# Norms with tokens on partitions, and another opening and ending of the last attention, in a fused four-block transformer kernel

## The reference, cut to what matters

```python
def _layernorm(x, axis=-1, eps=1e-05):
    m = jnp.mean(x, axis=axis, keepdims=True)
    v = jnp.var(x, axis=axis, keepdims=True)
    return (x - m) / jnp.sqrt(v + eps)
...
        Q = _l2norm(Qp)          # first attention: x / max(sqrt(sum x^2), 1e-12)
...
        # last attention, 16 heads of 8
        q = (query @ Wq + bq).reshape(B, Nq, H, D).transpose(0, 2, 1, 3)
        k = (key_value @ Wk + bk).reshape(B, Nkv, H, D).transpose(0, 2, 1, 3)
        v = (key_value @ Wv + bv).reshape(B, Nkv, H, D).transpose(0, 2, 1, 3)
        attn = jnp.einsum('bhqd,bhkd->bhqk', q, k) * scale
        attn = jnp.clip(attn, -CLAMP, CLAMP)
        attn = jax.nn.softmax(attn, axis=-1)
        attn = jnp.where(jnp.any(jnp.isnan(attn)), jnp.asarray(1.0 / Nkv, attn.dtype), attn)
        x = jnp.einsum('bhqk,bhkd->bqhd', attn, v).reshape(B, Nq, Cq)
        return x @ Wo + bo
```

## Time and profile before

| | us |
|---|---|
| median of the timed runs (three, 4366.15 to 4369.79) | 4366.79 |
| the profiled execution, its own time | 4373.3 |
| its span in the profile | 4371.7 |
| busy PE, DVE, ACT, POOL | 3678.5, 2638.5, 2052.6, 1419.1 |
| last attention, first clip to last copy | 3436.9 to 4284.0 |

### The profile page before, as it was taken

The page is one execution under the profiler, slowest core; times in us unless marked ns, Lnnn a source line. Parts: engine busy times, 40 slices in busy tenths (PEclk is TensorE's granted clock), DMA queues, the critical chain, the costliest instruction groups (busy, mean ns, idle before and its releaser), DMA issues. The chain is left out here.

```text
span 4371.7 us, 85152 instructions
## 1 busy us (share of the span) xinstructions
PE 3678.5 (84%) x32894; PEld 2444.3 (56%) x32894; DVE 2638.5 (60%) x3505; ACT 2052.6 (47%) x2955; POOL 1419.1 (32%) x1888
## 2 busy tenths in 40 slices
PE   7389999936279999988999997589777799989986
PEld 7267777613246666654666664267533366656663
DVE  8656666553244555425555543467545899989993
ACT  7267777701014344432443442266422477767763
POOL 0164555122422322212233220022102556656630
PEclk9689999968669999998999997799888799999997
DMA  6167777445132333312333320011001666666640
GB/s 168 49 154 171 179 170 174 116 162 213 33 78 68 84 86 84 86 48 66 89 87 83 87 68 22 29 49 47 1 18 32 147 151 153 152 141 154 151 112 15
DMA packets 197568, 434.50 MB, mean 99 GB/s; under 512 B 46219, under 2 KB 99389, under 8 KB 197100
## 3 DMA queue, kind: packets, MB, share of 16 engines
q1 hardware_dynamic: 122308, 339.43, 30.2%
q0 software_dynamic: 39424, 47.06, 5.1%
q10 hardware_dynamic: 35504, 43.39, 3.7%
HBM read 244.71 MB, written 32.67 MB: 63 GB/s over the span
## 5 line engine op out<-in xcount | busy, mean ns | idle before, releaser
L1482 DVE TENSOR_REDUCE L_mp<-ps 128x2 f32<-128x1000 f32 (+1 forms) x352 | 403.4, 1152 | 555.1 <-PE ps L1301 551.7
L1338 PE MATMUL ps<-L_p,L_cn 125*97 125x448 f32 x1536 | 639.4, 539 | 0.0
L1464 ACT ACTIVATE L_p<-ps 125x896 f32<-125x896 f32 x384 | 352.1, 917 | 607.6 <-PE ps L1326 536.0
L2158 ACT ACTIVATE L_p<-L_p 125x896 f32<-125x896 f32 x384 | 364.7, 950 | 236.0 <-DVE L_p L2211 232.2
L2194 DVE TENSOR_REDUCE L_mp<-ps 112x2 f32<-112x1000 f32 x384 | 455.4, 1190 | 7.3 <-PE ps L1971 7.3
L2211 DVE SCALAR_TENSOR_TENSOR L_p<-ps,xn 125x896 f32<-125x896 f32 x384 | 414.3, 1081 | 38.4 <-PE ps L1990 27.5
L1324 PE MATMUL ps<-L_qh,L_ch 97*125 97x448 f32 x768 | 386.0, 503 | 14.7 <-DMA L_qh<-L_mc 14.7
L1338 PEld LDWEIGHTS ps<-L_p,L_cn 125*97 125x97 f32 x1536 | 251.0, 163 | 199.2 <-issue 165.5
L1971 PE MATMUL ps<-L_ks,L_qs 96*128 96x500 bf16 x768 | 236.7, 393 | 79.1 <-DVE L_mp L2194 66.3
L1325 PE MATMUL ps<-L_ql,L_ch 96*125 96x448 f32 x768 | 284.4, 370 | 0.0
L1326 PE MATMUL ps<-L_qh,L_cl 96*125 96x448 f32 x768 | 282.7, 368 | 0.0
(11 more groups left out here) (533 smaller groups left out, 7353.4 us busy)
## 6 DMA issues: line engine op xcount, KB each, us to landing
L_ks<-L_k_part SPq DMA_DIRECT2D x288, 375.0 KB, 7.4
L_ks<-L_k_first SPq DMA_DIRECT2D x96, 375.0 KB, 6.3
moe_w<-in_L_w SPq DMA_DIRECT2D x64, 512.0 KB
L_cn<-in_ctxN SPq DMA_DIRECT2D x32, 568.4 KB
cs_ct<-in_ctxT SPq DMA_DIRECT2D x32, 562.5 KB, 4.3
L_raw<-in_ctxT SPq DMA_DIRECT2D x32, 562.5 KB, 5.0
L_cr<-in_ctxT POOLq DMA_DIRECT2D x32, 562.5 KB, 5.1
L_ch<-in_ctxT POOLq DMA_DIRECT2D x32, 562.5 KB, 4.6
```

The lines of the kernel that those rows point to most:

```text
L1338: mm = nc.tensor.matmul(U[:, a, :], CN[s][:, j, :], P[:, n % 2, a * HALF:(a + 1) * HALF], start=(j == 0), stop=(j == KT - 1))
L1464: nc.scalar.activation(two(P[:, n % 2, :]), SB[n % 2], ACT.Exp).then_inc(S["exped"].sem, 1)
L1482: nc.vector.tensor_reduce(mp[:, 2 * k:2 * k + n], ps[:, bank:bank + n, 0:500], AX.X, ALU.max).then_inc(S["chunk_maxed"].sem, 1)
L2158: nc.scalar.activation(two(P[0:KP, n % 3, :]), two(P[0:KP, n % 3, :]), ACT.Exp).then_inc(S["exped"], 1)
```

## The change

- `layer_norm`: the squares are summed with the tile of 112 tokens as stationary operand and one column of 1/128 moving, so that the sums stand with tokens on partitions, in 16 columns; root and reciprocal work on 112x16; 16 transposes of a column read as 128 columns spread it. A one-element square root stands before the squares. `fills` is work of GpSimd in the norm's block, `room` other tiles for its two big ones. `l2_norm_queries` likewise, with maximum and reciprocal once.
- Last attention: norm a3 runs inside `clipped_pass`, with SP's weights and first contexts (and one weight more, `WoN`) and GpSimd's fills of the ones rows and two `KS` tiles; the other two `KS` tiles lend their room to the norm and are filled in batches 0 and 1.
- Queries are made, scaled and split by quarters, the first quarter before the rest; keys of batch 0 go to three banks; keys of batch 1 are made before the values of batch 0. SP places the parts of batch 0's keys as they are ready, and three of the twelve pieces of its queries; `place_max(first)` stands before the load of batch 3's keys.
- `batches` writes all 32 bodies out.
- The uniform row: two products (mean context by `WVE`, that by `WO`) in the opening; at the end the count of bad rows and one masked copy that reads mask and row with repeated elements. `fold_values` and `uniform_if_nan` are gone.

```diff
@@ layer_norm
+        xc, x2 = room or (core.sb(f"{n}{tag}", [D, T], F32, ctx) for n in ("xc", "x2"))
+        sd = core.sb(f"sd{tag}", [TT, NT], F32, ctx)
+        rs = core.sb(f"rs{tag}", [TT, NT], F32, ctx)
...
-                    mm = nc.tensor.matmul(ps[G * c:G * (c + 1), 4, 0:CH], core.J[:, 0:G], x2[:, columns(c)],
-                                          start=True, stop=True)
+                    for t in range(per * c, per * (c + 1)):
+                        mm = nc.tensor.matmul(ps[0:TT, 4, t:t + 1], x2[:, t * TT:(t + 1) * TT], core.J[:, 0:1],
+                                              start=True, stop=True)
                 mm.then_inc(var.sem, 1)
                 pe.wait_ge(inv.sem, inv.at(1))
                 for c in range(NCH):
-                    nc.tensor.matmul(ps[:, c, 0:CH], core.ident[:, G * c:G * c + 1].to_broadcast([128, D]),
-                                     rs[:, :], start=True, stop=True).then_inc(spread.sem, 1)
+                    for k in range(per):
+                        t = per * c + k
+                        mm = nc.tensor.transpose(ps[:, c, k * TT:(k + 1) * TT],
+                                                 rs[:, t:t + 1].to_broadcast([TT, D]), core.ident[0:TT, 0:TT])
+                    mm.then_inc(spread.sem, 1)
...
+                nc.scalar.activation(warm[:, :], core.eps[0:1, :], ACT.Sqrt)
...
-                nc.scalar.activation(sd[:, :], ps[:, 4, 0:CH], ACT.Sqrt, bias=core.eps[:, :]).then_inc(std.sem, 1)
+                nc.scalar.activation(sd[:, :], ps[0:TT, 4, 0:NT], ACT.Sqrt, bias=core.eps[0:TT, :]).then_inc(std.sem, 1)
@@ l2_norm_queries
+                dve.wait_ge(nrm.sem, 1)
+                link(nc.vector.tensor_scalar(norm[:, :], norm[:, :], 1e-12, None, ALU.max))
+                nc.vector.reciprocal(inv[:, :], norm[:, :]).then_inc(inverted.sem, 1)
                 for c in range(NCH):
                     s = slice(c * CH, (c + 1) * CH)
-                    dve.wait_ge(nrm.sem, c + 1)
-                    link(nc.vector.tensor_scalar(x2[:, s], x2[:, s], 1e-12, None, ALU.max))
-                    link(nc.vector.reciprocal(x2[:, s], x2[:, s]))
-                    link(nc.vector.tensor_tensor(qn[:, s], qp[:, s], x2[:, s], ALU.mult))
+                    dve.wait_ge(spread.sem, c + 1)
+                    link(nc.vector.tensor_tensor(qn[:, s], qp[:, s], core.ps[:, c, 0:CH], ALU.mult))
@@ clipped_pass
-        for r in range(8):
-            body(Eight(None, r))
-        with eng.Fori(1, 3) as turn:
-            for r in range(8):
-                body(Eight(turn, r))
-        for r in range(24, B):
+        for r in range(B):
             body(Eight(None, r))
...
+    def loads(sp):
+        for dst, name in ((WQ[:, :], "WqP"), (WK[:, :], "WkP"), (WVE[:, :], "WvE"), (WOE[:, :, :], "WoE"),
+                          (WO[:, :], "WoN")):
+            sp.dma_start(dst, d[f"{L}_{name}"]).then_inc(S["w_in"], 16)
+        load_keys(sp, first)
+        load_values(sp, first)
+        sp.wait_ge(S["w_in"], 80)
+        sp.wait_ge(S["ck_in"], 16)
+        sp.wait_ge(S["cv_in"], 16)
+
+    def fills(pool):
+        for t in (CK, CV):
+            nc.gpsimd.memset(t[DC:KA, :], 1.0).then_inc(S["ones_row"], 1)
+        pool.wait_ge(S["ones_row"], 2)
+        for n in range(2):
+            ones_in_keys(pool, n)
...
+    norm(loads, fills, [KS[n][:, 0:2 * T].bitcast(F32) for n in (2, 3)])
...
+            load_keys(sp, first + 1)
+            place_part(first, 0)
+            sp.wait_ge(S["q_zeroed"], 4)
+            sp.wait_ge(S["q_split"], 1)
+            place_products(sp, first, 1, range(0, 3), "q_first")
+            place_part(first, 1)
+            place_part(first, 2)
+            load_keys(sp, first + 2)
             place_keys(first + 1)
-            load_keys(first + 3)
+            load_values(sp, first + 1)
             place_max(first)
+            load_keys(sp, first + 3)
             place_keys(first + 2)
...
+                if b.r < 2:
+                    pool.wait_ge(S["keys_third"], (b + 3).lin(3, 3))
+                    ones_in_keys(pool, b.r + 2)
...
+            make_queries(0)
             for c in range(3):
-                if c:
-                    pe.wait_ge(S["keys_copied"], c)
                 make_keys(first, c)
-            pe.wait_ge(S["keys_copied"], 3)
+            for c in range(1, NCH):
+                make_queries(c)
+            pe.wait_ge(S["mean_scaled"], 1)
+            nc.tensor.matmul(ps[:, 4, 0:B], WVE[:, :], mean[:, :], start=True, stop=True
+                             ).then_inc(S["mean_valued"], 1)
+            for c in range(3):
+                pe.wait_ge(S["keys_copied"], 3 + c if c else 1)
+                make_keys(first + 1, c)
+            pe.wait_ge(S["mean_copied"], 1)
+            nc.tensor.matmul(ps[:, 4, 64:64 + B], WO[:, :], mean_v[:, :], start=True, stop=True
+                             ).then_inc(S["mean_projected"], 1)
+            pe.wait_ge(S["keys_copied"], 6)
             for g in range(4):
...
             split_keys(first)
+            for c in range(3):
+                copy_keys(first + 1, c)
             for g in range(4):
                 copy_values(first, g)
-            split_keys(first + 1)
+            for c in range(3):
+                second_of_keys(first + 1, c)
...
+            dve.wait_ge(S["bad_counted"], 1)
+            link(nc.vector.tensor_copy(bad[:, :], ps[:, 6, 0:1]))
+            dve.wait_ge(S["out_copied"], B // 2)
+            link(nc.vector.copy_predicated(by_token(core.OT[:, :]), bad[:, 0:1].unsqueeze(2).to_broadcast([D, B, NQ]),
+                                           mean_out[:, :].unsqueeze(2).to_broadcast([D, B, NQ])))
```

More of the change, by code:

```diff
@@ L359, in l2_norm_queries @@
     w_in = core.sig("l2q_w_in")
-    mm1, qpd, sqd, mm2, nrm = (core.sig(f"l2q_{n}") for n in ("mm", "qp", "sq", "sum", "norm"))
+    mm1, qpd, sqd, mm2, nrm, inverted, spread = (core.sig(f"l2q_{n}") for n in (
+        "mm", "qp", "sq", "sum", "norm", "inverted", "spread"))
     with ExitStack() as ctx:
@@ L363, in l2_norm_queries @@
         x2 = core.sb("l2q_x2", [D, T], F32, ctx)
+        norm = core.sb("l2q_norm", [TT, NT], F32, ctx)
+        inv = core.sb("l2q_inv", [TT, NT], F32, ctx)
+        per = CH // TT
         with nc.Block() as block:
@@ L385, in _ @@
                     nc.scalar.activation(x2[:, s], qp[:, s], ACT.Square).then_inc(sqd.sem, 1)
-                act.wait_ge(sqd.sem, NCH)
-                for c in range(NCH):
-                    act.wait_ge(mm2.sem, c + 1)
-                    nc.scalar.activation(x2[:, c * CH:(c + 1) * CH], core.ps[:, 4 + c, 0:CH],
-                                         ACT.Sqrt).then_inc(nrm.sem, 1)
+                act.wait_ge(mm2.sem, 1)
+                nc.scalar.activation(norm[:, :], core.ps[0:TT, 4, 0:NT], ACT.Sqrt).then_inc(nrm.sem, 1)
             @block.vector
@@ L2159, in body @@
                                          ).then_inc(S["exped"], 1)
-            first = Eight(None, 0)
             def split_keys(b):
```

255 lines of the change are left out of this document (109 added, 146 removed).

## The result

The changed kernel takes 4267.19 us (median of four timed runs, 4259.11 to 4271.40) against 4367.81 us of the kernel before in the same session: ratio 0.9767, 95% interval 0.9752 to 0.9782. The forecast was 4262.5. The profiled execution took 4270.6 us (span 4269.0), 102.7 less than the one of before; the sum of terms said 104.3.

What follows compares the result with a forecast made beforehand. Stages between full barriers, VectorE bounding the last attention's batches; gains sought at the loop jump and short stages. Terms 13.5 + 28.5 + 9.6 + 27 + 25.7 = 104.3 us, from median 4366.79 to 4262.5; range 4236 to 4290.

Steps and rivals of the forecast that it cites:

- The deduction for slow sums: Norms: short products keep TensorE less busy, so some sums run at the low clock; 2.5 us taken off for all.
- rival 1: Norms and query norm: array stays at low clock through all sums and transposes; 20 us of gain lost, 4283; chance 0.17.
- the table load: Norms: moved ahead of the squares, where ScalarE waits, the 1.28 us load costs nothing and Sqrt no longer waits for it.
- the last MLP and the first weight fold: Stages behind norms: about eleven passes find a colder engine, 0.36 us a pass, 4 us lost.
- the forecast's steps: Query norm: sums 3.3 us, Sqrt 0.4, maximum and reciprocal 0.5, transposes and products 4.1; ends 175.7 to 176.5, -9.6 us.
- Rivals 2, 3 and 5: Opening gives 12, 4277.5 (chance 0.12); opening gives 38, 4251.5 (0.12); last attention's norm 10 us longer, 4272.5 (0.08).
- only 4 to 5 of these us are kept: Opening: row maximum goes out 7 to 9 us earlier, but batch 2's keys then end last; -27 for the whole opening.

Runs made afterwards that it cites:

- the dense products: Changed kernel plus unread 128x448 products in each norm, one between sums and transposes, two behind the transposes (none behind the last norm's): 4252.63 us, ratio 0.9728.
- both additions: Changed kernel with unread dense products both ahead of and behind each norm's transposes (none behind the last norm's): 4252.63 us, ratio 0.9728.
- the pair with the late maximum: Changed kernel against itself with batch 0's row maximum sent out behind the load of batch 3's keys again: 4265.84 us, ratio 0.9767.

## Why the prediction was right, and where not

The sum of terms came within 1.6 us of the two profiled executions, and in part that is luck: norms, query norm, loop, ending and other batches gave 6.1 us more than forecast, what follows the norms and the opening 7.7 less. The other 3.1 of the 4.7 us between forecast and median come from the step from a profiled execution to the median, 6.5 us before and 3.4 after.

**Loop.** Right in size and place: 14.1 against 13.5; the small rest is that the windows of the earlier trace rows are a cut of 26 us and the batch with the jump took 40.3. Both the trace and the run of the loop alone show no stall elsewhere in the longer code. The Trainium skill, "Runtime: NRT & Kernel Launch", section Instruction fetch mechanics, says that a taken branch outside the prefetched window forces a fetch before execution goes on; the trace agrees, with 14.1 us for this one jump over eight written-out batches. The run shows that the stall goes with the loop; that it is a fetch is the Trainium skill's account, and no run here shows it.

**Norms.** The terms inside a norm were right, summed over the eight. Sqrt starts 8.6 us later behind the means (0.14 to 2.66 a norm, 0.5 in the one shown; forecast 6.6, and 2.5 more for slow sums). Root and reciprocal, 0.25 as in the earlier trace rows, give 24.9 (forecast 24.8). From the reciprocal's end to the last product it is 4.0 us in seven norms and 3.3 in one (forecast 4.1), 19.5 less in all (forecast 17). So 35.8 us against 32.5. The deduction for slow sums was needed: 32 passes took 3.2 us in three of the eight norms and 3.3 to 4.3 in the others, 2.9 us more in all than at 3.2; rival 1's 5.4 did not come. Some of the later roots are slower means, too (4.94 us instead of 3.25 in a2), which the forecast didn't have. Part of the reasoning was wrong without harm: the table load is free in the new form wherever it stands (the run without the early root).

The step that failed is the price of what follows, 4 us for "the last MLP and the first weight fold" and 9.3 measured. For these two places it was right, 2.5 and 1.6. It left out the routers, 2.6 and 1.6 us. Its own rows showed the 32 router passes at 0.10 us in the stage right behind a norm, a price of the full clock (0.19 at the low one), and the clock had risen there during the eight wide spreading passes, which the change takes away. The cost stood in the neighbour, not in the changed lines: the run of the norms alone shows the same router groups with nothing else changed, and with the dense products they are back at 3.3 and 4.2 us.

The prediction cited the Trainium skill, "TensorE: Matmul & The Clock Gate", Part 4, that transposes don't count as busy for the clock. The traces agree so far as that in no run without a dense product ahead of them did the clock rise while the sixteen ran; with one ahead it did in some norms (with both additions, in the norm of the third stage, halfway through the sixteen). But in the norm shown the clock was already at 0.50 when the first of them ran, behind 32 one-column passes at 1.00 and a wait of 0.73 us, so they are not what lowered it there.

**Query norm.** 11.0 against 9.6: the forecast's steps (sums 3.46 us, root to reciprocal 0.75, transposes and products 4.0) hold and give 10.2 from the first sum on, the upper end of the forecast's range; the other 0.85 is that the sums start sooner behind norm a0 (its weights 0.5, the query products 0.35), which may be the execution's own.

**Opening.** Block start, first score and first score of batch 1 came within 1.4 us of the forecast, each for the reason given: GpSimd's fill ended last in the norm's block (3302.93 + 5.10 = 3308.03, 5.10 being the length of the earlier trace rows, against VectorE's 3306.30), a value copy before the first score, key parts before batch 1. Rivals 2, 3 and 5 are out with 24.6 us. The failed step is "only 4 to 5 of these us are kept" of the earlier row maximum. It is 0 by the pair with the late maximum, and at most 2.6 by the spread. The 2.4 us that are missing are the 4.5 of this step, less 0.9 found behind batch 1's first score, less 1.2 found ahead of it. The forecast saw that batch 2's keys end last and still gave the maximum a share: of two waits in a row, little or nothing is won at the one that ends first. It costed the two fills moved into batches 0 and 1 at nothing, at the end of GpSimd's list; there they do cost nothing (none of batches 1 to 29 is longer than 26.2 us), while a fill of the same size ahead of twelve transfers cost 4.5 us.

**Ending.** 26.2 against 25.7; the masked copy took the 2.14 us assumed, and the two products in the opening are not seen: TensorE waits 2.82 us for a context right behind the first.

## What to carry to other kernels

Price the clock of TensorE at the neighbours of an edit: list the short passes that start within a few microseconds behind it, and at which level they ran; if the edit replaces wide passes by narrow ones, they may lose up to a factor of two, and a few dense products into an unused bank can bring it back (14.6 us here for 25 added products around the narrow ones, 6.4 for the 16 behind them alone). Such products cost time of their own when they run at the low clock and the block waits for them.
Where several transfers are waited for one after the other, the last is the one to work on: reorder that one first, and read the gain of any other as zero until a run shows it. An engine's idle share in a steady stage says nothing on whether its queue can take one more instruction in the opening; name what stands behind it.

## What the runs showed of the hardware

- One jump back over eight written-out batches cost 14.1 us on the core, with ScalarE standing 6.3 us on "issue"; the same 32 bodies as straight code had no batch above 26.4 us.
- A product with a 128x112 tile as weights and one moving column took 0.10 us a pass at granted clock 1.00; a transpose of 112 columns in f32 0.10 at the full level and 0.19 at the low one.
- The same short passes ran at either level in kernels with the same code there. In norm a3 of the changed kernel the means took 4.87 us and the sixteen transposes 1.89; where only the order of SP's list differed, 3.24 and 3.25. How much of the spread between executions this makes is not shown: each kernel has one trace.
- A masked copy of 128x1792 that reads mask and data with repeated elements took 2.14 us, like one that reads them in full.
